# A decoder layer on one core: query rows by DMA, and a turn of 128 columns for the maxima

## The chip, the cores and the metric

The kernel runs on one core of one Trainium2 chip. PE (matmuls), DVE, ACT and POOL compute; SP issues the DMAs. The metric is the device time of one execution in microseconds.

## The reference

One pre-norm decoder layer on x of shape (8, 128, 128) in float32: self-attention, cross-attention to a context of the same shape, and a mixture of 64 experts.

```python
x = x + attn(layernorm(x), ...)         # 16 heads of 8; q and k through linear, conv and projection
x = x + xattn(layernorm(x), ctx, ctx, mask, Wq, bq, Wk, bk, Wv, bv, Wo, bo)
x = x + ffn(layernorm(x), ...)          # router: 4 of 8 groups, 8 of 64 experts; a shared expert

# self-attention
scores = einsum('bhqd,bhkd->bhqk', Q, K) / sqrt(DK)
scores = scores * tau[..., None] + delta[:, :, None, :]
out = einsum('bhqk,bhkd->bhqd', softmax(scores, axis=-1), V)
# cross-attention
scores = where(mask, -1e15, einsum('bhqd,bhkd->bhqk', q, k) / sqrt(HD))
```

Both softmaxes subtract the row maximum of the scores before the exponential.

## The kernel before

**Steps.** Attention runs as 16 steps (`STEPS`): step s is batch s % 8 of self-attention (s < 8, n = 0) or of cross-attention (n = 1). In a step there are four groups g of four heads j. Rows 32j to 32j+31 of a 128-partition tile belong to head j of a group. The first 8 of these (`S_MAX`) are for the maxima, the other 24 hold the 8 features of a head three times, as the high and low parts that make up a precise product.

`qst` and `kst[n]` hold query and key rows so stacked, of all batches. `kbd` and `qbd` are block-diagonal buffers with two slots, used by even and odd steps: in block j only rows 32j to 32j+31 are filled, the rest is zero.

**One step on the engines.**
1. `scores(s, g)` (PE, line 578): `qst` times `kbd` gives queries by keys, in the step before. `maximum` (DVE, 1211) reduces these to negated row maxima.
2. `split_max(s)` (DVE, 1217) writes each maximum as a high and a low part into columns of `negmax`.
3. `turn_max(s)` (PE, 598): a first matmul puts the query rows of all four groups through the identity into `bank[5]`, 512 columns (line 603). After `max_split` a second one adds the transposed `negmax`, repeated for the four groups, 512 columns (606). As rows 0 to 7 of each head are zero in `qst` and `negmax` is zero elsewhere, the bank then holds the queries with the maxima above them.
4. `queries_with_max(s)` copies that to the diagonal blocks of `qbd[:, s % 2]`, 32 rows by 512 a head: ACT (line 984) does three heads for s < 8 and two later, DVE (1225) the rest.
5. `scoresT(s, g)` (PE, 610): `kst` times `qbd` gives keys by queries with the maximum subtracted. `exponential` (ACT, 977), `pv` (PE, 623), `copy_o` (ACT), `turn_out` (PE), `norm` (DVE), `turn_on`, `project`, `add_residual` follow, partly a step or two later.

**The order** is written by hand; each engine goes through its own list of instructions in order and waits on semaphores. In step s PE issues `scores(s+1, 0)`, `turn_max(s)`, `scores(s+1, 1)`, `project(s-2)`, half of `pv(s-1)`, `scores(s+1, 2)`, the other half, and `scoresT(s, 0)` (lines 688 to 768). Steps 6 and 10 turn half the batches for the cross-attention queries, and steps 7 and 11 make them (`second_stack`), in a different order: `scores(8, 0)` then comes behind `scoresT(7, 1)`.

**SP** (line 345) issues all DMAs, in order. In its loop over s (416 to 431) it waits for `scored` of step s-2 and for the key rows, then issues four copies SBUF to SBUF of 32 partitions by 4 by 128 to `kbd[:, s % 2]` (line 427). Then comes `move_rows(s)` (383): from s = 2 to 5 `get_rows` brings stacked rows of batches 4 to 7 back from DRAM (line 373); at s = 6 `put_rows` stores the cross-attention keys there, at s = 7 and 9 `get_rows` fetches them into `kst[1]`. kbd of step 8 waits for the rows fetched at s = 7. Last are the loads of expert weights named in `PAIR_LOADS` (line 358). POOL splits these weights into parts (`early_weights`, 1746), pairs 11 to 16 once all query groups are stacked, and after pair 16 it normalises the inputs of the router, which PE turns at the end of step 14 (line 764, `turn_inputs(2, 0)`).

Of the kernel before, what the change touches and what calls it, by code (L numbers as in the profile page):

```python
# [5 lines left out]
F32 = mybir.dt.float32  # L6
# [55 lines left out]
def decoder_layer(nc, x, ctxT, mask, pack_a, pack_b, w3, rowsd, outT):  # L62
# [3 lines left out]
    with ExitStack() as ctx:  # L66
# [3 lines left out]
        def sem(name):  # L70
            return ctx.enter_context(nc.semaphore(name))
# [149 lines left out]
        rows_put = [sem(f"rows_put{i}") for i in range(3)]  # L221
        rows_got = [{lo // 2: sem(f"rows_got{i}_{lo}") for lo in los} for i, los in enumerate(((4, 6), (4, 6), (0, 4)))]
        kbd_ready = [sem(f"kbd_ready{i}") for i in range(2)]
        picks_ready = sem("picks_ready")
        kbd_first_high = sem("kbd_first_high")
        kbd_first = sem("kbd_first")
# [93 lines left out]
        def gelu_of(r, b):  # L320
            return gelu_half(r, 4 * (b // 4))[:, b % 4, :]

        def wait(eng, signal, value):

            if not isinstance(value, int) or value > 0:
                eng.wait_ge(signal, value)
# [18 lines left out]
        def _(sp):  # L345
# [37 lines left out]
            def move_rows(s):  # L383
# [19 lines left out]
                if s == 9:  # L403
                    get_rows(2, kst[1], 4, B, range(J))

            sp.wait_ge(kst_filled, G)
            get_maxima(0)
            get_maxima(4)
# [7 lines left out]
            for s in range(1, STEPS):  # L416
                n, b = s // B, s % B
                if s < 4:
                    sp.wait_ge(kst_ready, G)
                elif s < B:  # L420
                    sp.wait_ge(rows_got[0][2 if s < 6 else 3], 64)
                else:
                    sp.wait_ge(rows_got[2][b // 4 * 2], 64)
                    sp.wait_ge(maxima_got, 128)
                wait(sp, scored, G * (s - 1))
                for j in range(J):
                    sp.dma_start(kbd[32 * j:32 * j + 32, s % 2, :, j, :].bitcast(F32),
                                 kst[n][32 * j:32 * j + 32, :, b, :].bitcast(F32)).then_inc(kbd_ready[s % 2], 16)
                move_rows(s)
                for pair in PAIR_LOADS.get(s, ()):  # L430
                    load(pair)

            def coefficient_rows(n):

# [34 lines left out]
        def _(pe):  # L469
# [128 lines left out]
            def turn_max(s):  # L598

                wait(pe, qbd_high, s)  # L600
                wait(pe, qbd_ready, s)
                wait(pe, qst_odd, {8: 2, 12: 4}.get(s, 0))
                pe.matmul(bank[5][:, :], identr[:, :], qst[:, :, s % B, :], start=True, stop=False,  # L603
                          skip_group_check=True)
                pe.wait_ge(max_split, s + 1)
# [4 lines left out]
            def scoresT(s, g):  # L610
                n, b = s // B, s % B
                i = G * s + g
                if g == 0:
                    pe.wait_ge(qbd_high, s + 1)
                    pe.wait_ge(qbd_ready, s + 1)
                wait(pe, exped, i - 1)
                out = bank[2 + i % 2]
                if n == 1:
# [247 lines left out]
        def _(act):  # L866
# [116 lines left out]

            def queries_with_max(s):

                act.wait_ge(max_turned, s + 1)
                wait(act, scoredT, G * (s - 1))
                for j in range(J - 1 if s < B else 2):
                    r = slice(32 * j, 32 * j + 32)
                    last = act.activation(qbd[r, s % 2, :, j, :], bank[5][r, :].rearrange("p (g t) -> p g t", g=G),  # L990
                                          ACT.Copy)
                last.then_inc(qbd_high, 1)

            def expert_inputs(c, b):
# [111 lines left out]
        def _(dve):  # L1106
# [116 lines left out]
                                  cols[:, :, :, 0:1].bitcast(F32), ALU.subtract).then_inc(max_split, 1)  # L1223

            def queries_with_max(s):
                dve.wait_ge(max_turned, s + 1)
                wait(dve, scoredT, G * (s - 1))
                for j in range(J - 1 if s < B else 2, J):
                    r = slice(32 * j, 32 * j + 32)
                    last = dve.tensor_copy(qbd[r, s % 2, :, j, :], bank[5][r, :].rearrange("p (g t) -> p g t", g=G))  # L1230
                last.then_inc(qbd_ready, 1)

            def norm(s):
# [608 lines left out]
```

## Time and profile before

| | us |
|---|---|
| median of 3 runs | 303.44 (303.01 to 304.27) |
| profiled execution | 304.08 |
| its span, first to last instruction | 302.3 |
| busy: PE, DVE, ACT, POOL | 284.5, 228.2, 192.6, 184.0 |

The attention steps run from about 40 to 150 us of the span; before are the projections, behind are the experts, 66 units, in which PE works without a pause. The rows further down use these forms: a timeline row has start, duration, engine, line, operation, tiles (out<-in), shapes, a count, and in brackets the idle time before it and what ended it. A row with xN merges N instructions. Matmul durations overlap, so the pace of PE is read from starts. SPq rows are SP's DMA issues; a DMA lands later.

### The profile page before, as it was taken

How to read it: one execution, taken by the hardware profiler on the slowest of the kernel's cores; microseconds unless marked ns; L12 is line 12 of the kernel's file. 1: busy time of each engine (PE TensorE's matmuls, PEld its weight loads, DVE VectorE, ACT ScalarE, POOL GpSimd, SP SyncE). 2: the span in 40 equal slices, each digit the busy share in tenths (PEclk: the TensorE clock that was granted, in tenths of full speed). 3: DMA queues.
4: the chain of work that ended last, by engine and by line, in shares of the span. 5: the costliest groups of instructions: out<-in, count | busy, mean ns of one | idle time of the engine just before them, and what ended most of it. 6: DMA issues, size and time to landing. Idle time of an engine off the chain costs nothing.

```text
span 302.3 us, 5347 instructions
## 1 busy us (share of the span) xinstructions
PE 284.5 (94%) x1675; PEld 203.1 (67%) x1675; DVE 228.2 (76%) x512; ACT 192.6 (64%) x352; POOL 184.0 (61%) x262
## 2 busy tenths in 40 slices
PE   1999999999999999899889999999999999999994
PEld 1734576666655565456665788888888888888883
DVE  3896798799859886987896559789956676676664
ACT  2797747796884566456742797766655555555552
POOL 8240062097708870985177799999975665665661
PEclk9999989999999999999999999999999999999999
DMA  7920535457577243350000637666333353344321
GB/s 260 266 44 1 192 71 150 105 125 254 102 187 136 64 104 98 87 132 10 2 1 25 203 107 223 198 200 188 129 102 137 105 173 128 124 133 134 119 62 37
DMA packets 30636, 37.18 MB, mean 123 GB/s; under 512 B 5136, under 2 KB 19856, under 8 KB 30608
## 3 DMA queue, kind: packets, MB, share of 16 engines
q1 hardware_dynamic: 30608, 36.84, 42.2%
q8 instruction: 14, 0.23, 0.4%
q14 instruction: 14, 0.11, 0.1%
HBM read 28.43 MB, written 3.93 MB: 107 GB/s over the span
## 4 chain that ended last, share of the span: by engine, by line
PE 83%; DVE 9%; ACT 4%; DMA 2%; issue 2%; SPq 0%; ACTq 0%; DVEq 0%
PE bank L474 57%; PE bank L813 5%; PE bank L815 5%; PE bank L814 5%; PE bank L619 2%; PE bank L594 2%; PE bank L637 2%; DMA pa<-pack_a 2%; DVE rawmax L1214 2%; PE bank L606 1%; PE bank L480 1%; ACT conv L891 1%; PE bank L642 1%; PE bank L603 1%; ACT conv L922 1%
## 5 line engine op out<-in xcount | busy, mean ns | idle before, releaser
L1779 POOL TENSOR_TENSOR qbd<-vs,qbd 128x512 fp32r<-128x512 f32 x65 | 83.7, 1291 | 33.3 <-ACT qbd L1093 33.3
L474 PE MATMUL bank<-khl,stacks 128*128 128x512 f32 x396 | 101.4, 392 | 1.9 <-DVE vs L1575 1.9
L474 PEld LDWEIGHTS bank<-khl,stacks 128*128 128x128 f32 x396 | 73.6, 188 | 18.6 <-issue 3.7
L1606 DVE TENSOR_TENSOR conv<-bank,conv 128x512 f32<-128x512 f32 x60 | 41.5, 691 | 31.4 <-ACT bank L1057 28.3
L1057 ACT ACTIVATE bank<-bank 128x512 f32<-128x512 f32 x61 | 35.5, 582 | 43.9 <-PE bank L474 43.9
L1214 DVE TENSOR_REDUCE rawmax<-bank 128x4 f32<-128x512 f32 x64 | 43.3, 684 | 9.4 <-PE bank L474 8.4
L1093 ACT ACTIVATE qbd<-vs 128x512 fp32r<-128x512 f32 x65 | 40.6, 625 | 7.1 <-DVE vs L1583 4.6
L1614 DVE TENSOR_TENSOR vs<-conv,bank 128x512 f32<-128x512 f32 x61 | 41.9, 687 | 2.1
L474 PE MATMUL bank<-stacks 128*128 128x512 f32 x96 | 41.5, 482 | 1.1 <-DVE stacks L1524 0.6
L981 ACT ACTIVATE conv<-bank 128x512 f32<-128x512 f32 x64 | 35.1, 597 | 6.4 <-PE bank L474 5.6
L1743 POOL TENSOR_TENSOR stacks<-ring,stacks 128x384 fp32r<-128x384 f32 x33 | 33.7, 1021 | 1.4
L474 PE MATMUL bank<-qbd,stacks 128*128 128x512 f32 x64 | 30.3, 520 | 0.6 <-ACT conv L981 0.6
L990 ACT ACTIVATE qbd<-bank 32x512 fp32r<-32x512 f32 x40 | 23.4, 586 | 10.7 <-PE bank L606 10.4
L813 PE MATMUL bank<-qbd,stacks 128*128 128x512 f32 (+1 forms) x67 | 26.4, 394 | 0.7 <-POOL qbd L1779 0.6
L815 PE MATMUL bank<-qbd,stacks 128*128 128x512 f32 (+1 forms) x67 | 25.9, 387 | 0.0
L814 PE MATMUL bank<-qbd,stacks 128*128 128x512 f32 (+1 forms) x67 | 25.9, 386 | 0.0
L474 PE MATMUL bank<-conv,vs 128*9 128x128 f32 (+1 forms) x520 | 23.3, 279 | 0.3 <-ACT conv L922 0.3
L474 PEld LDWEIGHTS bank<-stacks 128*128 128x128 f32 x96 | 18.1, 194 | 6.4 <-issue 1.7
L969 ACT ACTIVATE oT<-bank 128x512 f32<-128x512 f32 x16 | 9.6, 597 | 15.2 <-PE bank L474 15.2
L1749 POOL CAST stacks<-ring 128x384 fp32r<-128x384 f32 x17 | 8.6, 504 | 17.2 <-ACT conv L981 9.5
L474 PEld LDWEIGHTS bank<-conv,vs 128*9 128x9 f32 (+1 forms) x520 | 12.4, 91 | 8.7 <-issue 5.7
L1230 DVE CAST qbd<-bank 32x512 fp32r<-32x512 f32 x24 | 16.7, 694 | 1.6 <-PE bank L606 1.0
(227 smaller groups left out, 431.6 us busy)
## 6 DMA issues: line engine op xcount, KB each, us to landing
conv<-coefficient_rows SPq DMA_DIRECT2D x122, 128.0 KB, 2.9
ring<-w SPq DMA_DIRECT2D x33, 192.0 KB, 3.6
stacks<-stacks SPq DMA_DIRECT2D x68, 64.0 KB, 2.1
split_rows<-stacks SPq DMA_DIRECT2D x6, 256.0 KB, 2.6
stacks<-split_rows SPq DMA_DIRECT2D x16, 96.0 KB
split_rows<-khl SPq DMA_DIRECT2D x3, 512.0 KB, 4.3
stacks<-split_rows SPq DMA_DIRECT2D x8, 192.0 KB
pa<-pack_a SPq DMA_DIRECT2D x1, 706.0 KB, 5.3
```

What stands on the lines that cost most here:

```text
L474: return pe.matmul(out, lhsT, rhs, start=start, stop=stop)
L813: pe.matmul(acc, whi(pair)[:, 2, :], hhi[:, w, cols], start=False, stop=False, skip_group_check=True)
L814: pe.matmul(acc, whi(pair)[:, 2, :], hlo[:, w, cols], start=False, stop=False, skip_group_check=True)
L815: pe.matmul(acc, wlo(pair)[:, 2, :], hhi[:, w, cols], start=False, stop=stop, skip_group_check=True).then_inc(down_done, 1)
L981: act.activation(probs[:, i % 8, :, :].rearrange("p j t -> p (j t)"), bank[2 + i % 2][:, :], ACT.Exp, scale=SCALE).then_inc(exped, 1)
L1057: act.activation(out, four(2 + p), ACT.Silu).then_inc(silu_done, 1)
L1093: act.activation(hhi[:, n % 4, :].rearrange("p (b t) -> p b t", b=4), hx[n % 4], ACT.Copy).then_inc(hhi_ready, 1)
L1214: dve.tensor_reduce(rawmax[:, s % 2, g, :].unsqueeze(2), bank[i % 2][:, :].rearrange("p (j k) -> p j k", j=J), AX.X, ALU.max, negate=True) ...
L1606: dve.tensor_tensor(out, gate, spread[:, n % ROWS, :, :], ALU.mult).then_inc(gate_scaled, 1)
L1614: dve.tensor_tensor(hx[n % 4], scaled[:, 4 * p:4 * p + 4, :], four(4 + p), ALU.mult).then_inc(h_done, 1)
L1743: pool.tensor_tensor(wlo(pair), ring[:, pair % RING, :, :], whi(pair).bitcast(F32), ALU.subtract).then_inc(wlo_ready, 1)
L1779: pool.tensor_tensor(hlo[:, n % 4, :].rearrange("p (b t) -> p b t", b=4), hx[n % 4], hhi[:, n % 4, :].bitcast(F32).rearrange("p (b t) -> p ...
```

## The change

- `turn_max(s)` for s > 0 no longer puts the query rows through PE. It waits for `max_split` and transposes `negmax` into 128 columns of `bank[5]`. Step 0 stays as it was.
- `queries_with_max(s)` for s > 0 copies only the 8 rows of the maxima a head; its source is the 128 columns, read four times by a broadcast (`turned`). The number of copies on ACT and DVE and their 512 elements a row stay.
- The 24 query rows a head reach `qbd` by four DMAs a step, SBUF to SBUF, 24 partitions by 4 by 128 each. SP issues them in `query_rows(s-1)`, in its loop of step s, behind the `kbd` copies of step s and ahead of `move_rows(s)` and the loads. It waits for the query rows to be there and for `scoredT` of step s-2, which frees the slot of `qbd`.
- `scoresT(s, 0)` waits for these (`qbd_rows`) too.

```diff
+        def turned(s, r):
+            if s == 0:
+                return bank[5][r, :].rearrange("p (g t) -> p g t", g=G)
+            return bank[5][r, 0:P].unsqueeze(1).broadcast_to([S_MAX, G, P])
...
+            def query_rows(s):
+                b = s % B
+                if s < 4:
+                    sp.wait_ge(qst_ready, G)
+                elif s < B:
+                    sp.wait_ge(rows_got[1][2 if s < 6 else 3], 64)
+                else:
+                    sp.wait_ge(qst_ready, G + 2 * (b // 4) + 2)
+                    sp.wait_ge(qst_odd, 2 * (b // 4) + 2)
+                wait(sp, scoredT, G * (s - 1))
+                for j in range(J):
+                    sp.dma_start(qbd[32 * j + S_MAX:32 * j + 32, s % 2, :, j, :].bitcast(F32),
+                                 qst[32 * j + S_MAX:32 * j + 32, :, b, :].bitcast(F32)).then_inc(qbd_rows[s % 2], 16)
...
+                if s > 1:
+                    query_rows(s - 1)
                 move_rows(s)
                 for pair in PAIR_LOADS.get(s, ()):
                     load(pair)
+            query_rows(STEPS - 1)
...
                 wait(pe, qst_odd, {8: 2, 12: 4}.get(s, 0))
+                if s > 0:
+                    pe.wait_ge(max_split, s + 1)
+                    mm(bank[5][:, 0:P], negmax[:, :], identr[:, :]).then_inc(max_turned, 1)
+                    return
...
                     pe.wait_ge(qbd_ready, s + 1)
+                    if s > 0:
+                        pe.wait_ge(qbd_rows[s % 2], 16 * J * ((s + 1) // 2))
...
+                rows = 32 if s == 0 else S_MAX
                 act.wait_ge(max_turned, s + 1)
                 wait(act, scoredT, G * (s - 1))
                 for j in range(J - 1 if s < B else 2):
-                    r = slice(32 * j, 32 * j + 32)
-                    last = act.activation(qbd[r, s % 2, :, j, :], bank[5][r, :].rearrange("p (g t) -> p g t", g=G),
-                                          ACT.Copy)
+                    r = slice(32 * j, 32 * j + rows)
+                    last = act.activation(qbd[r, s % 2, :, j, :], turned(s, r), ACT.Copy)
```

DVE's `queries_with_max` changes in the same way.

On PE, around turn_max of step 3, the program before has these rows (`turn_on(1)`, `scores(4, 0)`, the two matmuls of turn_max, `scores(4, 1)`, `project(1)`):

```order
L642 MATMUL bank<-pa,on 128x128
L474 MATMUL bank<-stacks 128x512
L603 MATMUL bank<-stacks,identr 128x512
L606 MATMUL bank<-identr,negmax 128x512
L474 MATMUL bank<-stacks 128x512
L474 MATMUL bank<-pa,onT 128x128
```

And in the changed program, where the lines have other numbers:

```order
L673 MATMUL bank<-pa,on 128x128
L499 MATMUL bank<-stacks 128x512
L499 MATMUL bank<-identr,negmax 128x128
L499 MATMUL bank<-stacks 128x512
L499 MATMUL bank<-pa,onT 128x128
```

One matmul is gone and the other has 128 columns; nothing else moves on PE.

SP's list before, in its loops of steps 6 to 9 (`stacks<-stacks` are the `kbd` copies, `split_rows<-khl` is put_rows, `stacks<-split_rows` get_rows, `ring<-w` the loads):

```order
L427 DMA stacks<-stacks 32x4x128 x4
L367 DMA split_rows<-khl 128x1024 x3
L427 DMA stacks<-stacks 32x4x128 x4
L373 DMA stacks<-split_rows 24x4x512 x4
L427 DMA stacks<-stacks 32x4x128 x4
L358 DMA ring<-w 128x384 x5
L427 DMA stacks<-stacks 32x4x128 x4
L373 DMA stacks<-split_rows 24x4x512 x4
```

And in the changed program (`qbd<-stacks` are the new copies):

```order
L449 DMA stacks<-stacks 32x4x128 x4
L425 DMA qbd<-stacks 24x4x128 x4
L374 DMA split_rows<-khl 128x1024 x3
L449 DMA stacks<-stacks 32x4x128 x4
L425 DMA qbd<-stacks 24x4x128 x4
L380 DMA stacks<-split_rows 24x4x512 x4
L449 DMA stacks<-stacks 32x4x128 x4
L425 DMA qbd<-stacks 24x4x128 x4
L365 DMA ring<-w 128x384 x5
L449 DMA stacks<-stacks 32x4x128 x4
L425 DMA qbd<-stacks 24x4x128 x4
L380 DMA stacks<-split_rows 24x4x512 x4
```

Four copies of query rows stand between the key copies of each step and what was behind these: the rows to and from DRAM and the loads. The third group of new copies here is that of step 7; it is behind the key copies of step 8.

## Rows read from the trace of the kernel before

**Rows 1.** The page, part 4: the chain of waits that ended last, by engine.
```profile
PE 83%; DVE 9%; ACT 4%; DMA 2%; issue 2%; SPq 0%; ACTq 0%; DVEq 0%
```

**Rows 2.** Timeline of PE around turn_max of step 5: start us, duration us, the rest.
```profile
71.42 0.33 PE L642 MATMUL bank<-pa,on 128*128 128x128 f32 x1
71.52 0.47 PE L474 MATMUL bank<-stacks 128*128 128x512 f32 x1
71.83 0.42 PE L603 MATMUL bank<-stacks,identr 128*128 128x512 f32 x1
72.09 0.40 PE L606 MATMUL bank<-identr,negmax 128*128 128x512 f32 x1
72.33 0.39 PE L474 MATMUL bank<-stacks 128*128 128x512 f32 x1
```

**Rows 3.** Groups by line and shape: count | busy us, mean ns | idle before.
```profile
L990 ACT ACTIVATE qbd<-bank 32x512 fp32r<-32x512 f32 x40 | 23.4, 586 | 10.7 <-PE bank L606 10.4
...
L1230 DVE CAST qbd<-bank 32x512 fp32r<-32x512 f32 x24 | 16.7, 694 | 1.6 <-PE bank L606 1.0
...
L969 ACT ACTIVATE oT<-bank 128x512 f32<-128x512 f32 x16 | 9.6, 597 | 15.2 <-PE bank L474 15.2
```

**Rows 4.** Timeline of DVE: maxima of step 10, then the first of step 11.
```profile
103.72 1.49 DVE L1214 TENSOR_REDUCE rawmax<-bank 128x4 f32<-128x512 f32 x2
...
106.57 0.69 DVE L1214 TENSOR_REDUCE rawmax<-bank 128x4 f32<-128x512 f32 x1 [0.56 <-PE bank L474]
```

**Rows 5.** Timeline of SP's DMA issues, from get_rows of s = 3 on.
```profile
49.95 1.77 SPq L373 DMA_DIRECT2D stacks<-split_rows  x4
52.43 2.52 SPq L427 DMA_DIRECT2D stacks<-stacks  x4
...
61.09 1.82 SPq L373 DMA_DIRECT2D stacks<-split_rows  x4
64.13 2.52 SPq L427 DMA_DIRECT2D stacks<-stacks  x4
66.76 1.84 SPq L367 DMA_DIRECT2D split_rows<-khl  x3
70.23 2.55 SPq L427 DMA_DIRECT2D stacks<-stacks  x4
73.03 2.23 SPq L373 DMA_DIRECT2D stacks<-split_rows  x4
80.65 2.52 SPq L427 DMA_DIRECT2D stacks<-stacks  x4
```

**Rows 6.** Lines 427, 373, 358: duration of an issue, ns min/median/max, and time to landing.
```profile
L427 SPq DMA_DIRECT2D stacks<-stacks x60: 585/601/1765, 37.1 to 130.5; - x60
...
DMA to landing us min/median/max: 2.0/2.1/4.6
...
L373 SPq DMA_DIRECT2D stacks<-split_rows x24: 369/376/1943, 45.4 to 90.8; - x24
...
L358 SPq DMA_DIRECT2D ring<-w x33: 425/584/2342, 3.8 to 207.9; - x33
...
DMA to landing us min/median/max: 2.5/3.6/7.7
```

**Rows 7.** Timeline of PE: the first scoresT of step 7.
```profile
86.97 0.50 PE L474 MATMUL bank<-qbd,stacks 128*128 128x512 f32 x1
```

**Rows 8.** Timelines of SP, DVE, POOL and PE, from step 11 to 14.
```profile
113.48 2.87 SPq L358 DMA_DIRECT2D ring<-w  x3
...
120.64 0.68 DVE L1498 CAST stacks<-bank 128x512 fp32r<-128x512 f32 x1
...
128.19 0.50 POOL L1749 CAST stacks<-ring 128x384 fp32r<-128x384 f32 x1
...
140.02 0.82 POOL L308 TENSOR_SCALAR xn<-xres,mv,nwt 128x128 f32<-128x128 f32 x1
...
142.41 0.60 PE L480 MATMUL bank<-pa,xn 128*128 128x128 f32 x4
```

**Rows 9.** Busy us (count) by engine, PE first, granted clock, DMA, in a stretch.
```profile
44.00:46.00 2.00, 2.00 (x11) 1.96 (x10) 1.97 (x7) 1.92 (x5) 1.94 (x2) 0.56 0.21 41
```

More of the change, by code:

```diff
@@ L223, in decoder_layer @@
         kbd_ready = [sem(f"kbd_ready{i}") for i in range(2)]
+        qbd_rows = [sem(f"qbd_rows{i}") for i in range(2)]
         picks_ready = sem("picks_ready")
@@ L1225, in queries_with_max @@
             def queries_with_max(s):
+                rows = 32 if s == 0 else S_MAX
                 dve.wait_ge(max_turned, s + 1)
@@ L1228, in queries_with_max @@
                 for j in range(J - 1 if s < B else 2, J):
-                    r = slice(32 * j, 32 * j + 32)
-                    last = dve.tensor_copy(qbd[r, s % 2, :, j, :], bank[5][r, :].rearrange("p (g t) -> p g t", g=G))
+                    r = slice(32 * j, 32 * j + rows)
+                    last = dve.tensor_copy(qbd[r, s % 2, :, j, :], turned(s, r))
                 last.then_inc(qbd_ready, 1)
```

## The prediction

> **What bounds the kernel now.** I read the chain of waits first: 83% of it is PE, so the first question is whether the changed step stands on PE's path [rows 1]. PE's timeline of one attention step shows the two matmuls of turn_max side by side with everything else [rows 2]. DVE's timeline then shows that PE is only half of the loop in this stage: between two steps DVE stops just once, for `scores(s+1, 0)`, and that matmul stands ahead of turn_max on PE [rows 4]. Last I read SP's own timeline, because the change puts all its new work there: from 45 to 73 us SP issues almost without a pause [rows 5]. That last view decides the forecast.
>
> I call the four `kbd` copies of line 427 kbd(s), the four new copies q(s), and what move_rows(s) issues m(s). Times are on the clock of the trace of before.
>
> **What PE saves.** Before, the two matmuls start at 71.83 and 72.09 and the next one at 72.33: 0.50 us for both [rows 2]. Afterwards there is one of 128 columns. The nearest row of 128 columns starts at 71.42 and its follower at 71.52, so 0.10 us [rows 2]. The bounds for the new matmul are that 0.10 and the 0.24 of a 512-column one. The saving is 0.40 us per step (0.26 at the least), in 15 steps (step 0 stays): 6.0 us if all were on the path.
>
> Most is not. In a step from 8 on, DVE runs on from its first maximum to `norm`, but for about 0.2 us inside two maxima (1.49 us, where one that follows a wait takes 0.69 and the next could follow by about 0.6), and the 0.56 us before the next step's first maximum [rows 4]. The 0.56 is spent on `scores(s+1, 0)`, which is issued before turn_max and doesn't move. So a plain step gains 0.2 us. Step 10 gains all 0.4, since there PE's end leads over ACT into the second query projection; step 8 gains 0.16, because its turn_max waits for `negmax` anyway and only the shorter second matmul counts; steps 7, 11 and 15 gain nothing, PE having slack there. For steps 8 to 10 that makes 0.2 + 0.16 + 0.4, about 0.7 us. What steps 1 to 6 and 12 to 14 could gain is lost in the waits below.
>
> **The copies on ACT and DVE.** They go from 32 rows by 512 to 8 rows by 512. The 32-row ones take 586 ns (ACT) and 694 ns (DVE); ACT's copy of 128 rows by 512 from the same kind of bank takes 597 [rows 3]. A quarter of the rows changed 2%, so I take 0 for both. If rows did count, ACT would win at most 40 x 0.59 us, but in these steps ACT idles anyway before its next copy. The source now repeats 128 columns four times; no row shows that, and I give it 0, with 0.1 us either way.
>
> **What SP pays.** Each loop of SP gets four more issues. No row shows an SBUF to SBUF copy of 24 rows, so I bound it: kbd's copies, SBUF to SBUF with 32 x 4 pieces, take 601 ns each; get_rows' copies, with just these 24 x 4 pieces but from DRAM, take 376 ns [rows 6]. With about 0.04 us between issues, four cost 2.6 or 1.7 us. I take three quarters of kbd's (96 pieces for 128) for the copy, 0.45 to 0.5 us, so q = 2.1 us for four. The copies land about 1.5 us after the last issue ends, as kbd's do (2.1 us from the start of an issue of 0.6) [rows 6].
>
> SP's spare time: the gaps over 0.2 us between m(3) and kbd(8) are 0.7 (51.7 to 52.4), 1.2 (62.9 to 64.1), 1.6 (68.6 to 70.2) and 0.25 (72.8 to 73.0), in sum 3.8 us [rows 5]. Ahead of m(7) come q(1) to q(6), 6 x 2.1 = 12.6 us. So m(7) starts 12.6 - 3.8 = 8.8 us later, at 81.8. (Its other condition, put_rows of m(6), moves by 5 x 2.1 - 2.0 = 8.5, from 66.8 to 75.2, and has 6.3 us until m(7): 81.5, not later.)
>
> On the way there PE already waits for keys. kbd(6) ends at 66.65 before and lands at about 68.2, when PE wants it at 71.5 [rows 2, 5]. It gets 4 x 2.1 = 8.4 us of new issues ahead of it less 1.9 us of gaps, so it lands at 74.7: 3 us late, and kbd(7) behind it somewhat more. These delays are inside the next one, not beside it.
>
> The longest one is q(7). It stands behind kbd(8), and kbd(8) waits for the key rows that m(7) fetches. Before, from the start of m(7) to the start of kbd(8) are 7.6 us (73.03 to 80.65) [rows 5]. That chain is now 81.8 + 7.6 = 89.4; kbd(8) 2.5, 91.9; q(7) 2.1, 94.0; landing 1.5, 95.5. PE wants q(7) for `scoresT(7, 0)`, at 86.97 before [rows 7]. Late by 8.5 us. With q = 1.7, m(7) is 6.5 us later and q(7) lands 5.9 late; with q = 2.6 it is 11.9. During that stall ACT finishes its earlier copies, so its first exponential starts at once: 0.3 us back.
>
> **A second wait, at the end of attention.** q(12) needs query groups that DVE finishes copying at 121.3, and the loads of expert pairs 13 to 15 are queued behind it; before, they were issued from 113.5 on [rows 8]. Now: q(12) 121.4 to 123.5, three loads 1.5 (their issues take 0.43 to 0.58 us [rows 6]), kbd(14) 2.6, q(13) 2.1, so the load of pair 16 is issued at 129.7 and lands 2.5 to 3.6 us later [rows 6], at 132.2 at the earliest. POOL splits pair 16 at 128.19 before: 4.0 us late. Behind it POOL normalises the inputs of the router, until 140.8, and PE turns these at 142.41 [rows 8]: it had 1.6 us to spare, so 2.4 us are lost (1.6 with q = 1.7; 4.5 with q = 2.6 and a landing of 3.6). This also eats what steps 12 to 14 save.
>
> **PE's clock.** At 44 to 46 us the granted clock is 0.56, that is mostly the lower level of 1.2 GHz, after a stretch in which PE waited for DVE [rows 9]. The stalls of 3 to 5 us could bring that back. Bounds: 0, and 1.7 us (half of 3.4 us). I take 0.5.
>
> **Sum.** 8.5 - 0.3 - 0.7 + 2.4 + 0.5 = +10.4 us. The profiled execution took 304.08 us for a span of 302.3; the median shown is 303.44, 0.6 less. The forecast against the median is 313.8 us. The low ends give 5.9 - 0.3 - 0.7 + 1.6 = +6.5 (309.9). The high ends give 11.9 - 0.3 - 0.7 + 4.5 + 1.7 = +17.1, and a long issue more (L427 has one of 1.77 us, L373 one of 1.94, in the same stretch [rows 6]) makes it 18.4 (321.8).
>
> The Trainium skill (DMA: Bandwidth & Descriptors, Rules for kernel authors) says under 64 KB a transfer is mostly overhead and should be joined to a larger one; these are 48 KB each. The landing of 2.1 us for 64 KB [rows 6] agrees. It bears on the price of q, not on the sum.
>
> **The rivals.**
> - Hidden and faster (0.07). SP issues ahead by a whole step, so the new copies could find room. Then only PE's saving counts: 0.7 for steps 8 to 10, 0.6 for steps 1 and 2 and 0.8 for 12 to 14, 2.1 us, 301.3 us; 297.4 if all 6.0 were on the path. For it: kbd lands some 3 us ahead of PE. Against it: it needs six groups in 3.8 us of gaps plus those 3 us, so 1.1 us a group, under 0.28 us an issue, and no 24-row issue is below 0.37 [rows 6]. That is the point from which it decides. The Trainium skill has a rule on this side (same page and section): issue early, compute, wait late, and the fixed cost overlaps. It holds for the landing; the trace says nothing for the issue, which is what runs short here.
> - Slower, but less (0.13): the return of the key rows is quicker than 7.6 us. For it: a load of 192 KB, also from DRAM, lands after 2.5 us at best and 3.6 in the median [rows 6]. Against it: these four are issued together and share the engines. With 3.5 us less, q(7) is 5 us late: 10.4 - 3.5 = +6.9, 310.3 us.
> - Slower still (0.20): the new issues cost what kbd's do, 0.6 us, and some long ones come on top: 318.5 us. The row nearest in kind (SBUF to SBUF, 512-byte pieces) speaks for it, the row with the same count against.
> - The change does nothing, or small gains and losses cancel: 303.4 us (0.02). SP would have to be almost free at 60 us, and it isn't.
>
> **How the numbers follow.** The forecast has 0.58, with its own range of 311 to 317. The measurement can't tell less than about 0.5% from no change. Faster by more than that: 0.06, nearly all of the first rival; within it 0.03; slower 0.91. For 8 in 10 the range takes in the weaker and most of the stronger case: 308 to 320.
>
> **What would show it.** In SP's timeline of the changed kernel, four issues with `qbd<-stacks` of 0.4 to 0.6 us each per step, no gap between 45 and 80 us, and m(7) at about 82. On PE: no L603 row after step 0; waits for DMA `stacks` (keys) of 1 to 3 us in steps 4 to 7; one wait of 4 us or more for `qbd<-stacks` at the first `scoresT` of step 7. At the end POOL waits for `ring<-w`. DVE's and ACT's `qbd` copies stay at 0.69 and 0.59 us. The stage after attention lasts as long as before. I am wrong in kind if PE waits for no DMA in steps 4 to 7, in size if the issue of a new copy lies outside 0.37 to 0.64 us or m(7)'s rows return in under 6 us.

## The result, and the profile after

The changed kernel takes 338.19 us (median of 4 runs, 337.17 to 340.2) beside 303.75 us for the kernel before on the same chip: a ratio of 1.1144, interval 1.1086 to 1.1202. The forecast of 313.8 us, and its range up to 320, lie far below. The profiled execution has a span of 335.4 us, 33.1 more than before, and a mean granted clock of 0.959.

The page's part 4 shows the kind of the loss at once. Where PE had 83% of the chain and SP nothing [rows 1], it now reads (after, shares of the span by engine):

```profile
PE 57%; SPq 19%; DMA 6%; DVE 6%; ACT 5%; issue 3%; POOL 3%; ACTq 0%; DVEq 0%; POOLq 0%
```

The waits of 40 to 190 us in the trace of after that name a DMA, or POOL's xn (engine, tile and line waited for, us in total, times, longest; a PEld and a PE row can be the same stretch of time). Before, PE waited for none of these:

```profile
PEld bank L499 <- DMA stacks<-stacks: 9.1, 5, 3.2
PE bank L499 <- DMA qbd<-stacks: 8.4, 4, 5.8
PE bank L499 <- DMA stacks<-stacks: 8.1, 5, 3.0
...
POOL stacks L1781 <- DMA ring<-w: 6.8, 2, 3.8
PEld bank L619 <- DMA stacks<-stacks: 6.0, 3, 4.4
...
PE bank L619 <- DMA stacks<-stacks: 5.4, 3, 4.2
...
PE bank L505 <- POOL xn L309: 2.7, 1, 2.7
...
PE bank L650 <- DMA qbd<-stacks: 1.7, 2, 1.1
```

The two copy lines of SP, duration of an issue in ns, min/median/max. L425 is the new one, L449 was L427 [rows 6]:

```profile
L425 SPq DMA_DIRECT2D qbd<-stacks x60: 778/803/1582, 43.5 to 170.5; - x60
```
```profile
L449 SPq DMA_DIRECT2D stacks<-stacks x60: 586/632/1426, 36.4 to 162.3; - x60
...
DMA to landing us min/median/max: 2.0/2.4/5.8
```

A new copy takes 803 ns to issue, not the 450 to 500 I had taken for it: q is 3.36 us for four. SP's own timeline of after, against [rows 5] (start us, duration us; L380 was L373, so the row at 90.05 is m(7), the one at 97.12 kbd(8), 100.67 q(7), 112.49 q(8), 115.89 m(9), 117.80 kbd(10)):

```profile
43.47 3.34 SPq L425 DMA_DIRECT2D qbd<-stacks  x4
46.85 1.80 SPq L380 DMA_DIRECT2D stacks<-split_rows  x4
48.76 2.62 SPq L449 DMA_DIRECT2D stacks<-stacks  x4
51.48 3.34 SPq L425 DMA_DIRECT2D qbd<-stacks  x4
...
86.65 3.36 SPq L425 DMA_DIRECT2D qbd<-stacks  x4
90.05 1.80 SPq L380 DMA_DIRECT2D stacks<-split_rows  x4
97.12 3.45 SPq L449 DMA_DIRECT2D stacks<-stacks  x4
100.67 3.35 SPq L425 DMA_DIRECT2D qbd<-stacks  x4
104.07 2.41 SPq L365 DMA_DIRECT2D ring<-w  x5
106.59 2.63 SPq L449 DMA_DIRECT2D stacks<-stacks  x4
112.49 3.36 SPq L425 DMA_DIRECT2D qbd<-stacks  x4
115.89 1.79 SPq L380 DMA_DIRECT2D stacks<-split_rows  x4
117.80 2.62 SPq L449 DMA_DIRECT2D stacks<-stacks  x4
```

No gap over 0.2 us is left from 43 to 91 us. PE's timeline of after shows the three longest waits, idle time and releaser in brackets: q(7) (at 86.97 before [rows 7]), kbd(10), and the router's last inputs (at 142.41 before [rows 8]):

```profile
105.76 0.76 PE L499 MATMUL bank<-qbd,stacks 128*128 128x512 f32 x1 [5.82 <-DMA qbd<-stacks]
...
125.03 0.42 PE L619 MATMUL bank<-maskb,identb 128*128 128x512 bf16 x1 [4.21 <-DMA stacks<-stacks]
...
173.99 0.33 PE L505 MATMUL bank<-pa,xn 128*128 128x128 f32 x1 [2.71 <-POOL xn L309]
```

Behind each of them PE runs slower for a while. Stretches of after (first figure: length in us, then busy us by engine; the granted clock is the third figure from the end): behind each of the three waits, and the stage after attention. Below 1.00 part of the stretch is at the lower of the two levels, 1.2 in place of 2.4 GHz:

```profile
106.20:112.20 6.00, 6.00 (x18) 4.02 (x18) 2.54 (x4) 2.50 (x5) 0.00 (x0) 0.55 0.60 167
...
125.00:129.80 4.80, 4.77 (x43) 2.86 (x43) 3.74 (x8) 1.32 (x3) 2.43 (x4) 0.64 0.39 79
174.00:180.00 6.00, 5.00 (x49) 3.38 (x49) 4.08 (x7) 3.29 (x8) 1.19 (x1) 0.72 0.01 3
183.90:326.00 142.10, 139.67 (x623) 112.73 (x624) 102.18 (x205) 85.46 (x155) 106.88 (x108) 1.00 0.43 132
```

ACT's and DVE's copies are as forecast (now 8 rows by 512; count | busy us, mean ns), against 586 and 694 [rows 3]:

```profile
L1022 ACT ACTIVATE qbd<-bank 8x512 fp32r<-8x512 f32 x37 | 21.7, 587 | 19.1 <-PE bank L499 18.8
...
L1262 DVE CAST qbd<-bank 8x512 fp32r<-8x512 f32 x23 | 16.0, 694 | 3.9 <-PE bank L499 3.4
```

To place the loss I took the start of each step's first exponential in both traces. This table is worked out from the timelines of ACT (the last column from PE's), in us:

| | step 7 | step 8 | step 9 | step 14 | step 15 | first expert matmul |
|---|---|---|---|---|---|---|
| before | 88.08 | 97.23 | 103.58 | 140.34 | 147.23 | 151.80 |
| after | 106.56 | 118.31 | 130.18 | 168.71 | 179.97 | 184.26 |
| later by | 18.5 | 21.1 | 26.6 | 28.4 | 32.7 | 32.5 |

So 18.5 us are gone by step 7, 2.6 more go to step 8, 5.5 to step 9, 1.8 on the way to step 14, and 4.4 in step 15. The start of attention isn't the same in all traces: the first exponential of step 0 is at 46.32 before and at 45.07 after, so counted from there 19.7 us are gone by step 7.

### The profile page after: what moved, and what is told of

The parts are those of the page before. It is cut to its first block, busy times and chain, and to the rows that moved or that the text cites. A ratio compares the mean times of both kernels' runs of the same rounds, so it can differ in the third digit from the quotient of the medians.

```text
span 335.4 us, 5408 instructions
## 1 busy us (share of the span) xinstructions
PE 288.5 (86%) x1660; PEld 204.6 (61%) x1660; DVE 228.1 (68%) x512; ACT 193.6 (58%) x352; POOL 184.0 (55%) x262
## 4 chain that ended last, share of the span: by engine, by line
PE 57%; SPq 19%; DMA 6%; DVE 6%; ACT 5%; issue 3%; POOL 3%; ACTq 0%; DVEq 0%; POOLq 0%
PE bank L499 39%; SPq L425 9%; SPq L449 6%; PE bank L844 4%; PE bank L846 4%; PE bank L845 4%; SPq L380 3%; DMA stacks<-split_rows 2%; DMA pa<-pack_a 2%; DMA stacks<-stacks 2%; PE bank L650 2%; PE bank L619 1%; ACT conv L922 1%; PE bank L505 1%; DMA ring<-w 1%
## 5 line engine op out<-in xcount | busy, mean ns | idle before, releaser
L499 PE MATMUL bank<-stacks 128*128 128x512 f32 x96 | 45.0, 527 | 9.3 <-DMA stacks<-stacks 8.1
L499 PE MATMUL bank<-qbd,stacks 128*128 128x512 f32 x64 | 32.0, 548 | 9.3 <-DMA qbd<-stacks 8.4
L1022 ACT ACTIVATE qbd<-bank 8x512 fp32r<-8x512 f32 (+1 forms) x40 | 23.5, 587 | 22.5 <-PE bank L499 18.8
L499 PEld LDWEIGHTS bank<-stacks 128*128 128x128 f32 x96 | 19.9, 212 | 16.3 <-DMA stacks<-stacks 9.1
L499 PE MATMUL bank<-conv,vs 128*9 128x128 f32 (+1 forms) x520 | 25.8, 304 | 0.8 <-ACT conv L953 0.8
L499 PEld LDWEIGHTS bank<-qbd,stacks 128*128 128x128 f32 x64 | 12.6, 207 | 14.3 <-issue 10.3
L499 PEld LDWEIGHTS bank<-conv,vs 128*9 128x9 f32 (+1 forms) x520 | 13.1, 97 | 10.7 <-issue 6.9
```

Of the source, the lines that this page charges most:

```text
L499: return pe.matmul(out, lhsT, rhs, start=start, stop=stop)
```

## The experiments

Times are medians of four executions, unless another number is given; a ratio is against the kernel before, run beside it on the same chip, with its 95% interval. Times of different experiments come partly from different chips.

**1. What a copy costs to issue (one execution).** The kernel before, with twelve shapes of copies at the end, four each, all landed before the next shape. `rows_of(lo, n)` copies n rows from partition lo, four pieces of 512 bytes in each.

```diff
+            copies(rows_of(32, 32))
+            copies(rows_of(40, 24))
...
+            copies(lambda probe, j: sp.dma_start(probe[40:64, 0, :], qst[40:64, 0, 0, :].bitcast(F32)))
...
+            copies(lambda probe, j: sp.dma_start(probe[40:64, :, :], split_rows[0, 0:24, 0, 512:1024].rearrange("p (g t) -> p g t", g=G)))
```

> The kernel before, with groups of four copies of one shape added behind its last store, each group waited for: SBUF to SBUF with 32, 24, 24, 16, 16 and 8 rows of four 512-byte pieces (the second, fourth and sixth start at row 40, the others at 32), 32 and 24 rows of one piece, 96 and 128 rows of four pieces, 24 rows of four pieces from DRAM, 24 rows of one 1024-byte piece. Theory A (the count of rows sets the issue: 24 rows are dearer than 32): 24 rows take 0.80 us from either start, 32 take 0.60, 16 take 0.4 or less. Rival B (the start inside a quadrant does it): 0.80 from row 40 and 0.45 from row 32. Rival C (SBUF as a source is dear for any shape but kbd's): everything but 32 rows lies near 0.8, and 24 rows from DRAM take 0.38. Its whole time is some 30 us over the kernel before and says nothing.

Issue times of single copies in ns, from the trace: 32 rows by 4 pieces 601 to 663; 24 by 4 from partition 40, 779 to 853; 24 from partition 32, 778 to 780; 16 rows 585 to 652; 8 rows 686 to 709. The later shapes stand in SP's timeline as groups of four (in order: 32 rows by 1 piece, 24 by 1, 96 by 4, 128 by 4, 24 by 4 from DRAM, 24 by one of 1024 bytes):

```profile
326.87 2.48 SPq L485 DMA_DIRECT2D qbd<-stacks  x4
330.56 3.09 SPq L486 DMA_DIRECT2D qbd<-stacks  x4
334.83 2.75 SPq L487 DMA_DIRECT2D qbd<-stacks  x4
340.31 2.76 SPq L488 DMA_DIRECT2D qbd<-stacks  x4
345.80 1.58 SPq L489 DMA_DIRECT2D qbd<-split_rows  x4
348.93 3.54 SPq L490 DMA_DIRECT2D xn<-stacks  x4
```

A quarter of the pieces saves nothing (24 rows by 1: 3.09 us for four), four times the rows cost almost nothing (128 by 4: 2.76), and the same 24 rows from DRAM cost half (1.58). Neither bytes, pieces nor the first partition set the issue; the number of rows and where the source is do. The sixth shape, 8 rows, is again dearer than 16. Of the three expectations A holds for 24 rows against 32 and misses on 16 (0.60, not 0.4 or less); B and C fall, by 24 rows from partition 32 and by 16 rows.

The Trainium skill (DMA: Bandwidth & Descriptors, Why a DMA increments its semaphore by 16 and not by 1) says that a DMA issued from SP goes over the largest number of engines, up to 16, that divides the slowest dimension of both sides, and that the issuing sequencer itself writes the semaphore's rest where fewer than 16 take part. Worked out by that rule, 24 rows go over 12 engines, 8 over 8, and multiples of 16 over all. The order of the SBUF figures fits that. The 24 rows from DRAM would have to pay it too, and take 0.38; that this is the cause isn't shown.

**2. No query copies.** The changed kernel without q(s), so the query rows of the buffer are not filled; GpSimd clears the slot once. It leaves the attention weights out. Not shown in the cut: DVE bounds the maxima, so that the exponentials stay finite, and ACT and DVE wait for the clearing in step 2.

```diff
-                if s > 1:
-                    query_rows(s - 1)
...
-            query_rows(STEPS - 1)
...
+            pool.memset(qbd[:, 0, :, :, :].bitcast(F32), 0.0).then_inc(rows_ready, 1)
```

> The changed kernel without the query copies and the wait for them. The query rows of qbd are zero from step 1 on (POOL clears slot 0 once, after step 0), and DVE bounds the maxima so that the exponentials stay finite: the attention weights are left out, all other work has its shape and order. If SP's queue is the whole cost: PE's saving of about 2 us is left, 301.4 us (300.5 to 302.5). Rival (the single turn, the broadcast source or the copies of 8 rows cost something themselves): 304 us or more. If PE's whole 6 us were on the path: 297.5.

307.45 us, ratio 1.0126 (1.0097 to 1.0155): not the 301.4 expected; by the number it is the rival's (304 or more). Step 1 alone loses about 4 us; from step 2 on to the experts the kernel gains 1.8 on the one before (its first exponential is 4.1 late in step 2, and the experts start 2.3 late; 0.76 of that in steps 8 to 10, 0.64 in 12 to 14, against the 0.7 and 0.8 of my terms). The split inside steps 8 to 10 is not as forecast: the first exponential of step 9 gains 0.4 on that of step 8, that of step 10 gains 0.2, that of step 11 nothing. PE's clock is part of the loss in step 1: PE waits 2.9 us for DVE's `negmax`, and behind that it is at the lower level for over 6 us:

```profile
50.40:57.00 6.60, 6.60 (x49) 4.59 (x49) 2.58 (x5) 3.41 (x6) 0.00 (x0) 0.50 0.19 56
```

That costs 3.3 us. The kernel before is at 1.00 from 46 to 57 us.

**3. The same, cleared later.**

```diff
                                    .broadcast_to([P, 4 * H, DK + 1]), ALU.mult).then_inc(values_scaled, 1)
+                if c == 0:
+                    pool.wait_ge(scoredT, G)
+                    pool.wait_ge(rows_ready, 3)
+                    pool.memset(qbd[:, 0, :, :, :].bitcast(F32), 0.0).then_inc(rows_ready, 1)
```

> The changed kernel without the four query copies per step: query rows are not filled (cleared once), so this part of the computation is left out. Against the run labelled e2 the one clearing of the buffer on GpSimd stands behind the first value scaling, not ahead of it. Theory (SP's issues are the whole loss; the rest of the edit saves what PE's path gains): the +4 us of e2 was the late first value product in step 1, so it goes, and 303.5 less 1.8 to 2.1 gives 301.5 us (300.9 to 302.3). Rival (the narrower copies or the broadcast source cost time on the path too): 303.5 to 307 us, with the first exponentials of steps 2 to 15 still 2 us or more late.

305.9 us (301.74 to 307.2, 10 executions), ratio 0.9998 (0.995 to 1.0045). The executions scatter (three of ten at 301.7 to 303.8, the others near 306), so the time proves little; the trace is of the longest, 307.2. In it the first exponential of step 1 is still 3.2 us late, so moving the clearing did not mend it; from step 2 to the experts the offset falls from 3.6 to 1.7 us. The first expectation holds for the pace of the steps after 1 and misses on the cause in step 1; the time and the early offsets lie where the rival has them. DVE's timeline, then GpSimd's, show what PE's wait of 2.2 us comes from: a small DVE instruction, 0.17 us in its median, takes 1.82 beside the memset. The lower clock follows here too (granted 0.50 from 50 to 56 us).

```profile
47.34 1.82 DVE L1251 TENSOR_SCALAR negmax<-rawmax 128x16 fp32r<-128x16 f32 x1
```
```profile
47.32 1.80 POOL L1758 MEMSET qbd<- 128x2048 f32 x1
```

What follows from both: without q(s) the rest of the edit gains 1.8 to 1.9 us from step 2 on, step 1 loses by the clearing, which the changed kernel doesn't have, and the whole loss of 34 us belongs to the copies.

**4. Copies that nobody waits for.** The kernel before, with q(s) issued at the changed kernel's places in SP's list, into a spare tile.

```diff
+                for j in range(J):
+                    sp.dma_start(qin[32 * j + S_MAX:32 * j + 32, 0:G, 0:P],
+                                 qst[32 * j + S_MAX:32 * j + 32, :, b, :].bitcast(F32)).then_inc(spare_got, 16)
...
+                if s > 1:
+                    query_rows(s - 1)
```

> The kernel before with the same 60 copies issued at the same places of SP's list, but into rows of a tile that is idle in this stage; no engine of the attention waits for them. If the issue time on SP is the cause, mostly through what is queued behind the copies: key copies and loads are as late as in the changed kernel, 330 us (325 to 337); only the waits for the query rows themselves are gone. Rival (the wait of scoresT for the query rows is the cause): under 315 us.

336.41 us, ratio 1.1071 (1.1038 to 1.1104). Nearly the whole loss is there, though no engine waits for these copies in the attention steps (ACT does once, behind the last): what is queued behind them on SP is late, not they themselves.

**5. q(7) ahead of kbd(8).** The changed kernel, one swap in SP's loop 8.

```diff
+                if s == B:
+                    query_rows(s - 1)
...
-                if s > 1:
+                if s > 1 and s != B:
                     query_rows(s - 1)
```

> The changed kernel, with the query copies of step 7 ahead of SP's wait for the fetched key rows instead of behind the key copies of step 8. They then run in the 5 us in which SP waits for these rows. The wait of 5.8 us of scoresT(7, 0) goes, but scores(8, 0) comes 1.3 us behind it and its keys don't land sooner: 4.5 us less than the changed kernel, 333.7 us. Rival (SP's list is bound again later, so that it is given back): 337 us or more. Had q(7) alone been the cause as forecast (its place behind the key copies of step 8), about 320 us.

331.62 us, ratio 1.0933 (1.0876 to 1.099): 6.6 us less than changed, where 4.5 were expected. Step 7's first exponential is 7.0 us earlier, of which 1.5 are scatter ahead of the swap (m(7) starts at 88.52 for 90.05). q(7) now goes out in the time in which SP waits for m(7)'s rows. This shows that the chain m(7), kbd(8), q(7) is the one that bounds step 7.

**6. 32 rows in place of 24.** As experiment 4, one third more bytes.

```diff
-                    sp.dma_start(qin[32 * j + S_MAX:32 * j + 32, 0:G, 0:P],
-                                 qst[32 * j + S_MAX:32 * j + 32, :, b, :].bitcast(F32)).then_inc(spare_got, 16)
+                    sp.dma_start(qin[32 * j:32 * j + 32, 0:G, 0:P],
+                                 qst[32 * j:32 * j + 32, :, b, :].bitcast(F32)).then_inc(spare_got, 16)
```

> The kernel before, and q(s) issued at the changed kernel's places into a tile that is used for nothing and that no one waits for, now with 32 rows a copy in place of 24 (e3 had 24 rows and 336.4 us). Theory (what counts is SP's time per issue, and the probe has 32 rows at 0.60 to 0.66 and 24 rows at 0.78 to 0.80 us): q falls from 3.36 to about 2.6 us although a third more bytes move, so m(7) comes 6 x 0.75 = 4.5 us earlier and the steps up to 9 two or three times q less: 318 us (314 to 322). Rival (the bytes or pieces on the DMA engines set the loss): 336 us or more.

328.75 us, ratio 1.0835 (1.0791 to 1.088), 7.7 us less than experiment 4: more bytes, less time. The rival (bytes) falls. The issue falls to the 0.60 us of the key copies:

```profile
L421 SPq DMA_DIRECT2D qin<-stacks x60: 585/601/1424, 43.5 to 158.9; - x60
```

But the number expected, 318, is missed by 11 us, and that is the more useful part. m(7) starts at 84.43, where my chain gives 73.0 + 6 x 2.56 - 3.8 = 84.6, so the arithmetic of the queue is right. The first exponential of step 8 is 12.7 us late, that of step 9 is 16.7, that of step 15 is 23.4: 4.1 us go in step 9 and 5.7 in step 15, of which my expectation had nothing.

**7. Two copies in place of four.** As experiment 4, with `for j in range(2)`.

```diff
-                for j in range(J):
+                for j in range(2):
                     sp.dma_start(qin[32 * j + S_MAX:32 * j + 32, 0:G, 0:P],
```

> As e3 (the kernel before, with copies of 24 rows into a tile for which no one waits), but only two of the four copies in each step. Theory: q = 2 x 0.82 = 1.65 us; by my own chain m(7) is 6 x 1.65 - 3.8 = 6.1 us late, and m(7) to kbd(8) 7.6 as before, so step 8 is about 6 late and the time 310 us (307 to 314): far less than half of e3's 33 us, since the gaps on SP take 3.8 us first and from step 9 on SP catches up. Rival (each copy has a price of its own, by contention on the DMA engines or in SBUF): half of 33, 320 us.

316.74 us, ratio 1.0419 (1.0366 to 1.0473): between the two expectations, so both miss. The trace decides where the time doesn't. kbd(8) starts at 87.60, 6.95 late (6.1 expected), the first exponential of step 8 is 7.8 late, of step 9 8.9, of step 15 10.8: the chain through m(7), and again a piece in steps 9 and 15 that I had left out. Half the copies cost 0.39 of the whole loss (12.7 of 33 us), which a fixed price per copy does not give.

**8. Queries from DRAM.** The changed kernel; q(4) to q(7) read the rows that the stage has stored there, same rows and bytes, same place on SP.

```diff
+                    rows = (stored_rows[j, :, :, P * b:P * b + P] if 4 <= s < B else
+                            qst[32 * j + S_MAX:32 * j + 32, :, b, :].bitcast(F32))
                     sp.dma_start(qbd[32 * j + S_MAX:32 * j + 32, s % 2, :, j, :].bitcast(F32),
-                                 qst[32 * j + S_MAX:32 * j + 32, :, b, :].bitcast(F32)).then_inc(qbd_rows[s % 2], 16)
+                                 rows).then_inc(qbd_rows[s % 2], 16)
```

> The changed kernel, with q(4) to q(7) read from the rows that the same stage has stored in DRAM and not from SBUF; same rows, same bytes, same place in SP's list. Theory (a DRAM source has 0.38 us an issue where the SBUF source has 0.82): q = 1.6 for these four, 4 x 1.75 = 7 us less ahead of the landing of q(7), three of them ahead of m(7), so m(7) 5.2 us earlier and the time about 331.5 us (329 to 334). Rival (the bytes, or the number of transfers in flight, are what counts): 338 us, no change.

331.19 us, ratio 1.0914 (1.0868 to 1.0959): as expected (331.5). In one kernel, two prices for one destination:

```profile
L428 SPq DMA_DIRECT2D qbd<-stacks x44: 778/792/1767, 43.4 to 162.8; - x44
L428 SPq DMA_DIRECT2D qbd<-split_rows x16: 369/384/540, 67.8 to 94.7; - x16
```

Together with experiment 6 this shows that SP's issue time, not the bytes moved, is what the kernel loses by.

**9. Loads of pairs 13 to 17 first.** The changed kernel.

```diff
+                if s in (13, 14):
+                    for pair in PAIR_LOADS.get(s, ()):
+                        load(pair)
                 if s > 1:
                     query_rows(s - 1)
                 move_rows(s)
-                for pair in PAIR_LOADS.get(s, ()):
+                for pair in PAIR_LOADS.get(s, ()) if s not in (13, 14) else ():
```

> The changed kernel, with the loads of pairs 13 to 17 in SP's loops 13 and 14 ahead of q(12) and q(13), not behind them. Theory (the second wait of the prediction): the load of pair 16 is issued at 153.7 and not 158.7 us, so POOL's chain of 12.6 us ends at 169.0, ahead of PE, which turns the last inputs at 171.3; PE's wait of 2.7 us and its lower clock behind it (about 0.9) go, 334.7 us (334 to 336). Rival (the last 6 us of attention come from late keys or queries): q(13) moves only 0.5 us, 337.5 us or more.

332.16 us, ratio 1.0944 (1.09 to 1.0988): 6.0 less than changed, 3.5 expected (334 to 336). From the first exponential of step 14 to that of step 15 it is 6.9 us, as before, and not 11.3. PE's wait for `xn` is gone and the clock stays up there: 2.7 us of wait bring 4.4. The other 1.6 us are scatter: this trace is 2.1 us earlier than that of the changed kernel at step 7 already (104.43 and 106.56), where the two programs are the same. So a difference of 2 us between two of these slower kernels proves nothing by itself; the way from step to step does.

**10. m(9) ahead of q(8).** The changed kernel.

```diff
+                if s == 9:
+                    move_rows(s)
                 if s > 1:
                     query_rows(s - 1)
-                move_rows(s)
+                if s != 9:
+                    move_rows(s)
```

> The changed kernel, with what move_rows(9) issues ahead of q(8), not behind it. In the trace of the changed kernel SP stands 3.3 us at q(8), which needs the second half's queries, and only then comes m(9) (1.8 us) and kbd(10), for which PE waits 4.2 us at 125.0. Theory (kbd(10) behind q(7), q(8) and m(9) in SP's order is what steps 8 and 9 lose, a term that the prediction lacked): m(9) goes into the 3.3 us, kbd(10) starts 1.9 us earlier and lands alone, so 335.5 us (334.5 to 336.5). Rival (these steps lose on the queries, or on PE's clock): 338 us, no change.

332.02 us, ratio 1.0922 (1.0892 to 1.0952): 6.2 less than changed, 2.7 expected (334.5 to 336.5). From step 8 to step 9 it is 5.94 us in place of 11.87. SP's timeline of this kernel, with m(9) at 109.97 and kbd(10) at 116.42, for which PE no longer waits:

```profile
107.31 2.62 SPq L449 DMA_DIRECT2D stacks<-stacks  x4
109.97 1.83 SPq L380 DMA_DIRECT2D stacks<-split_rows  x4
112.95 3.36 SPq L425 DMA_DIRECT2D qbd<-stacks  x4
116.42 2.60 SPq L449 DMA_DIRECT2D stacks<-stacks  x4
```

Counted from step 7's first exponential, kbd(10) starts 2.1 us earlier, and yet 5.9 us go, 4.2 of wait and 1.7 of slow clock. The rest is the landing. For kbd(10)'s four copies the changed kernel, where they are issued right behind m(9), and then this one, where they are not, have:

```profile
DMA to landing us min/median/max: 4.8/5.3/5.8
```
```profile
DMA to landing us min/median/max: 2.1/2.1/2.1
```

In the traces of experiments 4, 6 and 7 kbd(10) is right behind m(9) too, and the medians are 5.7, 6.1 and 5.4; in the kernel before it is 1 us behind, with 4.3. PE wanted the keys at 120.8 in the changed kernel, and the last copy was issued at 119.81: landing in 2.1 us it would have been 1.1 us late, not 4.2 (an estimate from these rows). So about 3 of the 4.2 us are the slow landing and the rest the place in the list. Why copies right behind these rows land late isn't shown.

**11. The new way in steps 9, 10, 13 and 14 alone (12 executions).** The kernel before where SP is full, the changed one where it has gaps of 3 us or more.

```diff
+        NEW = (9, 10, 13, 14)
...
-            if s == 0:
+            if s not in NEW:
                 return bank[5][r, :].rearrange("p (g t) -> p g t", g=G)
...
-                if s > 1:
+                first = s in (14,)
+                if s - 1 in NEW and not first:
                     query_rows(s - 1)
```

> The kernel before, with the change in steps 9, 10, 13 and 14 alone, where SP has gaps of 3 us and more, and in loop 14 the loads ahead of q(13). Theory: 3.4 us for q fits each gap, so nothing waits and only PE's saving stays, 0.2 us in steps 9, 13 and 14 and 0.4 in step 10: about 1.0 us less than before, 302.4 to 303.0 us. Rival (the copies disturb keys, rows or loads in flight even in gaps, or the saving of PE is no saving): 303.5 to 306 us.

In loop 14 the loads go ahead of q(13), which the cut doesn't show. 303.23 us beside 303.62, ratio 0.9977 (0.996 to 0.9993): faster than both kernels, than the one before by 0.4 us in the medians and 0.7 by the ratio, for 1.0 expected (302.4 to 303.0). Its trace has the four copies in gaps, q(9) and q(10) here, and from step 8 to the experts 1.2 us less than before:

```profile
94.61 3.34 SPq L427 DMA_DIRECT2D qbd<-stacks  x4
98.06 2.60 SPq L451 DMA_DIRECT2D stacks<-stacks  x4
100.78 3.33 SPq L427 DMA_DIRECT2D qbd<-stacks  x4
104.15 0.52 SPq L367 DMA_DIRECT2D ring<-w  x1
```

The gain is clear of no gain, though small. The saving on PE is real, and four copies of 3.4 us together cost nothing where SP has room for them.

**12. The edits of 8, 9 and 10 together.** SP's loop now reads, beside the DRAM source of experiment 8:

```diff
+                if s == 9:
+                    move_rows(s)
+                if s in (13, 14):
+                    for pair in PAIR_LOADS.get(s, ()):
+                        load(pair)
                 if s > 1:
                     query_rows(s - 1)
```

> The changed kernel with the edits of e8, e9 and e10 together: q(4) to q(7) from DRAM, pairs 13 to 17 ahead of q(12) and q(13), m(9) ahead of q(8). Against the changed kernel they gave 0.0230, 0.0200 and 0.0222 of the time of before, one by one. Theory (three separate places in SP's list: ahead of m(7), ahead of kbd(10), ahead of pair 16): the gains add, 1.1144 - 0.0652 = 1.049 of before, 318.5 us (316 to 321), and what is left is q(1) to q(3) and the rest of q ahead of m(7) and kbd(8). Rival (they take from one reserve, SP's total of issues): the sum is not reached, 323 us or more.

320.34 us, ratio 1.0557 (1.0497 to 1.0616), inside the 316 to 321 expected; the sum of the single gains gave 1.049, just below the interval. They add up nearly, so they are three separate places of one list. What is left, 16 us, is mainly ahead of step 7 (11.6 us late there).

## Why the prediction was wrong

- **The mechanism and the sign were right.** SP's list bounds the changed kernel, m(7), kbd(8) and q(7) are its chain (experiments 4 and 5), the loads of pairs 13 to 17 are the second wait (9), and PE, ACT and DVE give and take what was worked out (experiment 2: 0.8 us in steps 8 to 10 for 0.7, though the parts were given to the wrong steps, so that their sum came out is partly luck).
- **The step that failed is the price of q: 2.1 us for four, and 3.36 measured.** I had bounded a 24-row copy by the two nearest rows, 376 and 601 ns, and scaled between them by pieces. Both halves of that were wrong. The real one, 803 ns, lies outside both bounds, and outside the 0.37 to 0.64 us that I had named as the sign of being wrong in size, and pieces don't set it: 24 rows are dearer to issue than 32 (experiments 1 and 6), and an SBUF source is dearer than DRAM with the same shape (experiments 1 and 8). The 376 was the same shape with the other source, the 601 the same source with another row count; neither bounds the pair.
- **With the right price the chain holds.** 6 x 3.36 - 3.8 = 16.4 later gives m(7) at 89.4 (90.05 measured), kbd(8) at 97.0 (97.12), and q(7) landing at about 104.4, 17.4 late for 8.5 (18.5 by the exponentials). The tail by the same formula: two more q cost 2 x 1.26, so 2.4 becomes 4.9. That makes +21.8 us or 325.2, and explains 11.4 of the 24.4 us by which I missed. In the tail PE waits only 2.7 of the 4.9 for `xn`; it had itself lost 2.5 us from step 12 to step 14 (15.24 for 12.71). With q = 1.7 the formula gives q(7) 5.7 late, not the 5.9 of my low end.
- **A term was missing: kbd(10).** I looked for the longest chain up to step 7, and took it that afterwards SP has room. q(8) stands ahead of m(9) and kbd(10) in SP's list and needs the second half's queries, for which SP stood 3.3 us (109.2 to 112.5). I had seen this pattern for q(12), not for q(8). It is 5.9 us, 1.7 of clock among them (experiment 10). At the 2.56 us of experiment 6 it is already 4.1. And I had taken one landing for all key copies, 2.1 us, though [rows 6] have one of 4.6, which is a copy of kbd(10) itself: behind m(9) the four took 4.8 to 5.8, which is about 3 of these 5.9 us.
- **The clock was mis-sized: 0.5 us taken, about 6 measured**, outside my bound of 1.7. That bound is what the one such stretch of the kernel before costs, by [rows 9] and the row ahead of it (2 x 0.41 + 2 x 0.44):

```profile
42.00:44.00 2.00, 1.85 (x5) 1.13 (x6) 1.77 (x6) 0.33 (x1) 1.04 (x1) 0.59 0.35 69
```

The changed kernel has three that count. Behind the wait for q(7) the granted clock is 0.55 for 6 us, mostly 1.2 GHz; that loses 6 x 0.45 = 2.7 us, and the way from step 7 to 8 takes 11.75 us for 9.15. Behind kbd(10) it is 4.8 x 0.36 = 1.7, behind `xn` 6 x 0.28 = 1.7. Each stall costs again 0.4 to 0.6 of its own length, and I had put 0.5 us against all of them. Ahead of step 7 the clock is low as well (0.50 from 87.7 to 94.5), but there SP's list sets the time, as the chain above shows.
- **The rest**, 1.8 us on the way from step 9 to 14 (waits for keys and queries of 0.5 to 1.1 us in steps 13 and 14, less what PE saves) and 0.6 us after attention (from the first expert matmul to the end of the span, 151.1 for 150.5), has no experiment of its own.
- The strongest rival, slower still by the price of the key copies (318.5), was nearer, and experiment 6 is that case: at 0.6 us a copy, and without anyone waiting for it, 328.75. So even the right neighbour would have missed by 10 us, for want of the terms for kbd(10) and for the clock.

## What to carry to other kernels

Before work is moved to an in-order DMA queue, the queue's own timeline has to be read to the end of the stage, with every issue that stands behind the new one and everything the new one waits for; price an issue by a row with the same row count and the same kind of source, and where none is there keep the upper bound open. The three long stalls of PE here were paid 1.4 to 1.6 times, since its clock was lower behind them, and copies issued right behind large loads landed in 5 us where 2 is usual. Where the new issues fall into gaps of the queue the saving stays: apply such a change step by step of the schedule, not to all steps.

## What the runs showed of the hardware

- SP's issue time for an SBUF to SBUF copy: 0.60 us for 16 or 32 rows, 0.65 for 96 or 128, 0.69 for 8, 0.78 to 0.80 for 24 (0.71 to 0.78 with one piece a row in place of four). From DRAM into the same 24 rows: 0.38.
- A copy of 64 KB, SBUF to SBUF, lands 2.1 us after its issue begins where nothing large is ahead of it, and 4.8 to 5.8 right behind four loads of 192 KB (kbd(10), experiment 10 and the changed kernel).
- A DVE instruction of 128 by 16 elements takes 0.17 us, and 1.82 beside a GpSimd memset of 1.80 us that began 0.02 us before it. In experiment 2 the same DVE instruction takes 1.61 us and ends with the memset (48.73 and 48.69). The Trainium skill (SBUF — State Buffer, SBUF: two separate sides) names one port pair that GpSimd and some forms of DVE's operations (those in a mode that uses both port pairs, or with two inputs in SBUF while GpSimd reads there) hold in turn for a whole instruction. These rows agree with such a hold; whether this DVE instruction ran in one of these forms no run here shows.
